# Remainders of the attention's weights on GpSimd: four instructions of 128 columns in place of one of 512

## The chip, the cores and the metric

One NeuronCore of a Trainium2 chip runs the whole program. The metric is the device time of one execution in microseconds (us); less is better. The engines are called as in the profile: PE (TensorE, the matmuls; PEld is its loading of weights), DVE (VectorE), ACT (ScalarE), POOL (GpSimd) and SP (SyncE, which issues DMAs).

## What is computed

Four layers work on x of 4 x 256 tokens with 256 features. Each adds to x an FFN of a conditioned input; the last one's FFN is a whole transformer block with attention over 16 heads of 128 and a mixture of experts. The part around the change is the attention of that layer:

```python
h = rmsnorm(x, ln1_w)
q = (h @ wq).reshape(b, s, H, HD)
k = (h @ wk).reshape(b, s, H, HD)
v = (h @ wv).reshape(b, s, H, HD)
scores = jnp.einsum('bqhd,bkhd->bhqk', q, k) / np.sqrt(HD).astype(np.float32)
scores = jnp.where(causal, scores, jnp.float32(-1000000000.0))
attn = jax.nn.softmax(scores, axis=-1)
ao = jnp.einsum('bhqk,bkhd->bqhd', attn, v).reshape(b, s, H * HD) @ wo
x = x + ao
```

## The kernel before

Activations lie with features on the 128 partitions and the 1024 tokens along the columns. The kernel is a chain of blocks, one for each stage: layer 0 (NF4 weights), layer 1 (experts chosen by sorting), layer 2 (ternary weights), the conditioning of layer 3, and `layer3`, which holds attention and experts. The order of each engine's work is written out by hand, and the engines wait for one another by counts on semaphores.

In `layer3` each product of weight and activation is taken in three passes of a reduced f32 format: high part times high part, high times low, low times high. So each weight matrix exists three times in SBUF: RAW as loaded, WH its rounded copy, WL the remainder RAW - WH; the activations as XH and XL. The attention runs over 8 groups of two heads (GROUPS). A group's weights are 4 parts of GCOL = 512 columns (for q, k, v and the output), and RAW, WH and WL have two slots, so that group g + 1 is prepared while g is computed:

- SP loads RAW of group g (L2143) once the remainders of group g - 2 are made.
- ACT rounds a part into WH (`split_high`, L2194), between its evacuations of the projections C4, C6, C8, C10 (when n is 4, 6, 8, 10, parts 0 to 3).
- POOL makes the remainder of the part (`split_low`, L2166) when ACT has counted it on w_high, and counts on w_low. POOL has nothing else to do in the groups.
- PE waits for the whole group on w_low before the first projection of it (`project`, n = 0, step D0 of the group before).

The steps of a group come from the list PLAN, read by all engines in the same order; a step's number is the unit (a head and a batch) or the projection:

```python
PLAN = """S0 C4 S1 N0 C5 C6 N1 T0 C7 S2 C8 T1 A0 N2 S3 C9 A1 T2 N3 C10 A2 T3 C11 A3
    S4 D0 S5 N4 D1 S6 N5 T4 D2 S7 N6 T5 A4 D3 N7 T6 A5 P0 T7 A6 P1 A7 W0 W1 W2 W3""".split()
```

C and D are projections: PE fills bank n % 2 (L2432 for V, L2441 for Q and K), which ACT (n even, L2209) or DVE (n odd, L2291) copies out; the next projection of the same bank waits for that. S is the scores (PE L2474, L2475), their masked row maximum on DVE (L2306, then nm at L2310) and the exponentials on ACT (L2226). N is the scaling into PN on DVE, in two instructions (L2319). T transposes PN on PE (L2482), and ACT copies the result to PT (L2234). A is the product with V (L2493, L2495), split into AH on ACT (L2242) and AL on DVE (L2325). P and W are the output projection (L2450), added to XC on DVE (L2331).

The last group makes no attention weights: POOL and ACT split the first expert's weights instead (`ex.split_low`, L1941), into the same RAW, WH and WL. The class Packed, which runs the experts, is told at which counts of w_low and wo the two slots are free. In layer 0, POOL scales HALF (L432) and multiplies EKV (L440) while DVE makes STEP (L573) and runs scans (L201, L203).

Of the kernel before, what the change touches and what calls it, by code (L numbers as in the profile page):

```python
# [13 lines left out]
F32 = mybir.dt.float32  # L14
F32R = mybir.dt.float32r
BF16 = mybir.dt.bfloat16
ALU = mybir.AluOpType
# [100 lines left out]
def chunk(t, j):  # L118

    return halves(t)[:, bass.ds(j * W, W)]  # L120
# [1511 lines left out]
GROUPS = HEADS // 2  # L1632
GCOL = 512
# [93 lines left out]
def later(g):  # L1727

    return not isinstance(g, int) or g >= 1
# [23 lines left out]
def made(g, n):  # L1753
    return LAST_MADE[n] if is_last(g) else n
# [303 lines left out]
def layer3(nc, k, io):  # L2058

    scale = float(HD) ** -0.5  # L2060
    with ExitStack() as ctx:
        def sb(name, shape, dt):
            return ctx.enter_context(nc.sbuf_tensor(name, shape, dt))

        def sem(name):
# [6 lines left out]
        RAW = sb("RAW3", [P, 2, 4 * GCOL], F32)  # L2072
        WH = sb("WH3", [P, 2, 4 * GCOL], F32R)
        WL = sb("WL3", [P, 2, 4 * GCOL], F32R)
# [28 lines left out]
        r_in, logits, rt, ex_, cw_turned, rows, sent, owned, summed, stored = [  # L2103
            sem(n + "_4") for n in ("r_in", "logits", "route", "exps", "turned", "rows", "sent", "owned", "summed", "stored")]
        ex = Packed(nc, k, sb, sem, io["l3_experts"], routed_d, (XH, XL), (RAW, WH, WL),
                    (w_low, [4 * (GROUPS - 1), 4 * GROUPS]), (wo, [4 * (GROUPS - 1), 4 * GROUPS]))

        with nc.sbuf_tensor("Q3", [P, 2, T], F32) as Q, nc.sbuf_tensor("K3", [P, 2, T], F32) as K:
            pass
# [25 lines left out]
        @block.sync  # L2135
        def _(sp):
            sp.dma_start(tiles.LN[:], io["l3_ln"]).then_inc(ln_in, 16)
            for g in range(2):
                sp.dma_start(RAW[:, g], io["l3_attn"][g]).then_inc(raw_in[g], 16)
            for g in range(2, GROUPS):  # L2140

                sp.wait_ge(w_low, 4 * (g - 1))
                sp.dma_start(RAW[:, g % 2], io["l3_attn"][g]).then_inc(raw_in[g % 2], 16)  # L2143
            sp.dma_start(RW[:], io["l3_router"]).then_inc(r_in, 16)
            sp.dma_start(routed_d[EXPERTS3:].rearrange("o (a b) -> (o a) b", b=P), k.ONES[0:T // P]).then_inc(sent, 16)
            ex.load_raw(sp, 0)
            ex.load_raw(sp, 1)

            sp.wait_ge(rows, 2)
            sp.dma_start(routed_d[0:EXPERTS3], ROWW[:]).then_inc(sent, 16)  # L2150
            sp.wait_ge(sent, 32)
            ex.load_tw(sp, 1)
            ex.load_rest(sp)
            for n, j in enumerate(ORDER):

                sp.wait_ge(summed, n + 1)
                sp.dma_start(io["out"][:, j * W:(j + 1) * W], chunk(k.X[:], j)).then_inc(stored, 16)

            sp.wait_ge(stored, 16 * NCH)

        def split_low(pool, g, slot):
            for m in range(4):

                pool.wait_ge(w_high, 4 * g + (m + 1))
                c = slice(m * GCOL, (m + 1) * GCOL)
                pool.tensor_tensor(WL[:, slot, c], RAW[:, slot, c], WH[:, slot, c].bitcast(F32),  # L2166
                                   ALU.subtract).then_inc(w_low, 1)

        @block.gpsimd
        def _(pool):  # L2170
            pool.memset(MASK[:], 0.0).then_inc(mask, 1)
            pool.wait_ge(mask, 1)

            pool.affine_select(out=MASK[:], in_=MASK[:], compare_op=ALU.is_ge, fill=NEG,
                               base=P, pattern=[[-1, 2 * P]], channel_multiplier=1).then_inc(mask, 1)
            split_low(pool, 0, 0)
            pool.memset(ex.TW[:, 0], 1.0).then_inc(ex.tw_one, 1)

            def body(g, u, r):
                if not is_last(g):  # L2180
                    split_low(pool, g + 1, 1 if u is None else u)

            each_group(pool, body)
            for part in range(3):
                ex.split_low(pool, 0, part)
            ex.gpsimd(pool)
# [220 lines left out]
        def _(pe):  # L2407
# [5 lines left out]
            def project(g, slot, n):  # L2413
                s = n % 2
                c = made(g, n)
                if n == 0:

                    pe.wait_ge(w_low, 4 * (g + 1))
                if not later(g) and n < 2:

                    pe.wait_ge(norm.xl, 2 * (n + 1))

                if n in (4, 5) and later(g):
                    pe.wait_ge(added, 4 * g - 5 + n)
                elif n >= 2 or later(g):
                    pe.wait_ge(evac[s], 6 * g + n // 2)
                if 4 <= c < 8:
                    for t in (2 * (c - 4), 2 * (c - 4) + 1):
                        passes = [(h, x, w) for h in range(KD) for x, w in ((XH, WH), (XL, WH), (XH, WL))]
                        for i, (h, x, w) in enumerate(passes):  # L2430
                            at = 2 * GCOL + h * 2 * HD
                            mm = pe.matmul(banks[s][:, (t % 2) * 2 * HD:(t % 2 + 1) * 2 * HD],  # L2432
                                           x[:, h, t * P:(t + 1) * P], w[:, slot, at:at + 2 * HD],
                                           start=(i == 0), stop=(i == len(passes) - 1))
                else:
                    head, c2 = (0, c) if c < 4 else (1, c - 8)
                    half = c2 % 2
                    passes = [(h, x, w) for h in range(KD) for x, w in ((XH, WH), (XL, WH), (XH, WL))]
                    for i, (h, x, w) in enumerate(passes):
                        at = (c2 // 2) * GCOL + (h * 2 + head) * HD  # L2440
                        mm = pe.matmul(banks[s][:], w[:, slot, at:at + HD], x[:, h, half * W:(half + 1) * W],  # L2441
                                       start=(i == 0), stop=(i == len(passes) - 1))
                mm.then_inc(proj, 1)
# [10 lines left out]
            def body(g, u, r):  # L2454
                slot = 0 if u is None else (1 + u) % 2
                for kind, n, to in steps_of(g):
# [3 lines left out]
                    if kind == "C":  # L2460
                        project(to, slot if n >= 4 else 1 - slot, n)
# [64 lines left out]
            for n in range(4):  # L2526
                project(0, 0, n)
# [44 lines left out]
def build(nc, io):  # L2572
    with ExitStack() as kept:
        k = Kit(nc)
        make_kept(nc, k, lambda name, shape, dt: kept.enter_context(nc.sbuf_tensor(name, shape, dt)))
        k.banks = [kept.enter_context(nc.psum_tensor(f"bank{i}", [P, W], F32)) for i in range(8)]
        with ExitStack() as ctx:
            make_gain(nc, k, lambda name, shape, dt: ctx.enter_context(nc.sbuf_tensor(name, shape, dt)),
                      lambda name: ctx.enter_context(nc.semaphore(name)))
            layer0(nc, k, io)  # L2580
            make_ternary(nc, k, lambda name, shape, dt: ctx.enter_context(nc.sbuf_tensor(name, shape, dt)))
            layer1(nc, k, io)
            layer2(nc, k, io)
            layer3_cond(nc, k)
        layer3(nc, k, io)
# [78 lines left out]
```

## Time and profile before

| | us |
|---|---|
| median of 3 runs | 931.06 |
| lowest and highest | 929.69, 932.71 |
| the profiled execution | 930.3 |
| its span, first to last instruction | 928.6 |
| PE busy | 777.7 (84%) |
| DVE busy | 576.0 (62%) |
| ACT busy | 415.5 (45%) |
| POOL busy | 237.6 (26%) |

The busy times are sums over the span, over stages with different limits. The attention's groups lie between about 384 and 696 us of the span. Starts in the rows below are in us from the span's start. The name in brackets behind an idle time is what ended it.

### The profile page before, as it was taken

What the parts mean: (1) busy time and instruction counts of PE and PEld (TensorE: products, weight loads), DVE (VectorE), ACT (ScalarE), POOL (GpSimd) and SP (SyncE); (2) the same over time, 40 slices, a digit from 0 to 9 for tenths busy, and PEclk for the clock granted to TensorE, in tenths of its full rate; (3) what the DMA queues carried; (4) which work ended last, traced back from release to release, by engine and by line L of the source; (5) the groups of instructions that cost most, each with busy time, mean ns of one, the idle gap of its engine ahead of it and who ended that gap; (6) DMA issues with size and microseconds to landing.
All of it is one profiled execution on the core that took longest, in us unless ns stands there. A gap on an engine that the chain in (4) does not pass through costs nothing.

```text
span 928.6 us, 11225 instructions
## 1 busy us (share of the span) xinstructions
PE 777.7 (84%) x3628; PEld 580.5 (63%) x3633; DVE 576.0 (62%) x1269; ACT 415.5 (45%) x857; POOL 237.6 (26%) x245
## 2 busy tenths in 40 slices
PE   1986695887865466999999999999979799999997
PEld 0433453544532145878788787887758688888885
DVE  6998899889989882555555556555555133332323
ACT  6894212244414555554463554635444233434332
POOL 5210101401042422102011020110102355555554
PEclk9998897889887777899999999999999999999999
DMA  4000004724120002110010110101000523224421
GB/s 144 1 1 1 0 0 173 313 64 142 40 80 0 1 1 90 46 46 22 26 47 1 46 34 14 35 1 34 1 1 1 139 62 109 57 76 95 103 52 46
DMA packets 37230, 49.84 MB, mean 54 GB/s; under 512 B 18526, under 2 KB 29894, under 8 KB 35510
## 3 DMA queue, kind: packets, MB, share of 16 engines
q1 hardware_dynamic: 36118, 46.90, 16.2%
q0 software_dynamic: 768, 2.10, 0.7%
q8 instruction: 30, 0.49, 0.2%
q14 instruction: 26, 0.21, 0.1%
q10 hardware_dynamic: 288, 0.14, 0.1%
HBM read 42.99 MB, written 6.13 MB: 53 GB/s over the span
## 4 chain that ended last, share of the span: by engine, by line
PE 47%; DVE 6%; ACT 4%; issue 2%; DMA 1%; POOL 0%; DVEq 0%; SPq 0%; ACTq 0%
PE bank L1958 15%; PE bank L1974 7%; PE bank L2441 6%; PE bank L2432 5%; PE bank L2450 4%; PE bank L2475 3%; PE bank L2493 2%; PE bank L2482 2%; PE bank L2474 1%; DVE EX L2306 1%; ACT EX L2226 1%; PE bank L2495 1%; DVE PN L2319 1%; ACT AH L2242 1%; ACT PT L2234 1%
## 5 line engine op out<-in xcount | busy, mean ns | idle before, releaser
L2013 DVE TENSOR_TENSOR B_l<-bank,TW_l 128x512 f32<-128x512 f32 (+1 forms) x50 | 34.4, 690 | 138.6 <-PE bank L1958 129.2
L2226 ACT ACTIVATE EX<-EX,nm 128x128 f32<-128x128 f32 (+1 forms) x128 | 57.5, 450 | 109.3 <-DVE nm L2310 108.6
L2046 POOL TENSOR_TENSOR HL_l<-H_l,HH_l 128x512 fp32r<-128x512 f32 (+1 forms) x50 | 65.2, 1306 | 145.1 <-ACT HH_l L2024 145.1
L2166 POOL TENSOR_TENSOR WL<-RAW,WH 128x512 fp32r<-128x512 f32 x32 | 41.0, 1287 | 228.2 <-ACT WH L2194 228.2
L1958 PE MATMUL bank<-XH,WH 128*128 128x512 f32 (+1 forms) x200 | 80.3, 401 | 3.1 <-ACT ROWW L2274 1.7
L1958 PE MATMUL bank<-XL,WH 128*128 128x512 f32 (+1 forms) x200 | 80.3, 402 | 0.0
L1958 PE MATMUL bank<-XH,WL 128*128 128x512 f32 (+1 forms) x200 | 80.2, 401 | 0.0
L2033 ACT ACTIVATE S_l<-bank 128x512 f32<-128x512 f32 (+1 forms) x50 | 29.8, 597 | 85.4 <-PE bank L1958 85.3
L2325 DVE TENSOR_TENSOR AL<-bank,AH 128x256 fp32r<-128x256 f32 x64 | 27.1, 424 | 60.6 <-ACT AH L2242 60.6
L155 POOL TENSOR_TENSOR WV<-EUK,V 128x512 f32<-128x512 f32 x16 | 23.7, 1486 | 151.8 <-DVE GAIN L244 117.0
L2441 PE MATMUL bank<-XH,WH 128*128 128x512 f32 x128 | 59.3, 463 | 1.3 <-DVE XL L1716 1.3
L1941 POOL TENSOR_TENSOR WL<-RAW,WH 128x512 fp32r<-128x512 f32 x39 | 50.7, 1300 | 32.4 <-ACT WH L1935 32.4
L2306 DVE CUSTOM_DVE_ANT_0 EX<-bank,MASK 128x128 f32<-128x128 f32 (+1 forms) x128 | 40.6, 355 | 25.6 <-PE bank L2475 25.3
L2441 PE MATMUL bank<-XH,WL 128*128 128x512 f32 x128 | 51.3, 400 | 0.0
L2441 PE MATMUL bank<-XL,WH 128*128 128x512 f32 x128 | 51.1, 399 | 0.0
L2024 ACT ACTIVATE HH_l<-H_l 128x512 fp32r<-128x512 f32 (+1 forms) x50 | 31.7, 634 | 40.8 <-PE bank L1974 34.4
L1958 PEld LDWEIGHTS bank<-XH,WH 128*128 128x128 f32 (+1 forms) x200 | 38.3, 191 | 13.1 <-ACT ROWW L2274 2.0
L474 ACT ACTIVATE MARK<-SC,THR 128x1536 bf16<-128x1536 bf16 (+1 forms) x30 | 43.1, 1512 | 6.2 <-PE bank L687 6.2
L2319 DVE TENSOR_SCALAR PN<-EX,rr 128x128 f32<-128x128 f32 (+1 forms) x128 | 43.3, 381 | 2.3
L1974 PE MATMUL bank<-HH_l,WH 128*128 128x512 f32 (+1 forms) x100 | 39.7, 397 | 5.9 <-POOL HL_l L2046 5.9
L1958 PEld LDWEIGHTS bank<-XH,WL 128*128 128x128 f32 (+1 forms) x200 | 38.2, 191 | 9.1
L1958 PEld LDWEIGHTS bank<-XL,WH 128*128 128x128 f32 (+1 forms) x200 | 38.1, 190 | 9.2
(298 smaller groups left out, 2079.3 us busy)
## 6 DMA issues: line engine op xcount, KB each, us to landing
RAW<-l_attn SPq DMA_DIRECT2D x8, 1024.0 KB, 4.8
WE<-l_experts SPq DMA_DIRECT2D x1, 6144.0 KB, 23.5
RAW<-l_experts SPq DMA_DIRECT2D x9, 512.0 KB, 3.8
TW_l<-routed SPq DMA_DIRECT2D x16, 256.0 KB, 5.1
RAW<-l_w SPq DMA_DIRECT2D x3, 1024.0 KB
TW_l<-routed SPq DMA_DIRECT2D x14, 192.0 KB, 3.1
RAW<-l_experts SPq DMA_DIRECT2D x9, 256.0 KB, 4.2
sorted_x<-ZERO SPq DMA_DIRECT2D x1, 1920.0 KB, 8.9
```

The source lines that it names most:

```text
L474: act.activation(MARK[:, n % RING, 0:cols], SC[:, at:at + cols], ACT.Sign, bias=THR[:, i:i + 1]).then_inc(mark, 1)
L1941: pool.tensor_tensor(self.WL[:, i % 2, c], self.RAW[:, i % 2, c], self.WH[:, i % 2, c].bitcast(F32), ALU.subtract).then_inc(self.w_low, 1)
L1958: mm = pe.matmul(self.k.banks[2 * (q % 2) + o][0:rows], w[:, i % 2, at:at + rows], x[:, h, n * W:(n + 1) * W], start=(s == 0), stop=(s == ...
L1974: mm = pe.matmul(self.k.banks[4 + 2 * m + n][:], w[0:rows, i % 2, at:at + P], x[0:rows, q % 4], start=((i, f, s) == (0, 0, 0)), stop=(q >= ...
L2046: pool.tensor_tensor(self.HL[0:rows, q % 4], self.H[0:rows, q % 2], self.HH[0:rows, q % 4].bitcast(F32), ALU.subtract).then_inc(self.h_low, 1)
L2166: pool.tensor_tensor(WL[:, slot, c], RAW[:, slot, c], WH[:, slot, c].bitcast(F32), ALU.subtract).then_inc(w_low, 1)
L2226: act.activation(EX[:, s, a:b], EX[:, s, a:b], ACT.Exp, bias=nm[:, s, i:i + 1], scale=scale, accum_out=rs[:, s, i:i + 1]).then_inc(expd, 1)
L2306: v.tensor_tensor_reduce(EX[:, s, a:b], banks[2 + s][:, a:b], MASK[:, 2 * P - (b - a):], 1.0, NEG, ALU.add, ALU.max, accum_out=mx[:, s, i: ...
L2319: v.tensor_scalar(PN[:, s, a:b], EX[:, s, a:b], rr[:, s, i:i + 1], None, ALU.mult).then_inc(normed, 1)
L2432: mm = pe.matmul(banks[s][:, (t % 2) * 2 * HD:(t % 2 + 1) * 2 * HD], x[:, h, t * P:(t + 1) * P], w[:, slot, at:at + 2 * HD], start=(i == 0 ...
L2441: mm = pe.matmul(banks[s][:], w[:, slot, at:at + HD], x[:, h, half * W:(half + 1) * W], start=(i == 0), stop=(i == len(passes) - 1))
L2450: mm = pe.matmul(banks[n % 2][:], w[:, slot, at:at + P], x[:, head, half * W:(half + 1) * W], start=(head == 0 and i == 0), stop=(head == ...
```

## The change

`split_low` of `layer3` goes over each part in four instructions of QCOL = 128 columns, each counting on w_low, in place of one of 512. All who wait for w_low of the attention wait for four times the count: SP's loads of RAW, PE's first projection of a group, and the experts' first loads. The experts' own `split_low` (L1941) stays with 512 columns, as do ACT's `split_high` instructions.

```diff
         ex = Packed(nc, k, sb, sem, io["l3_experts"], routed_d, (XH, XL), (RAW, WH, WL),
-                    (w_low, [4 * (GROUPS - 1), 4 * GROUPS]), (wo, [4 * (GROUPS - 1), 4 * GROUPS]))
+                    (w_low, [16 * (GROUPS - 1), 16 * GROUPS]), (wo, [4 * (GROUPS - 1), 4 * GROUPS]))
...
-                sp.wait_ge(w_low, 4 * (g - 1))
+                sp.wait_ge(w_low, 16 * (g - 1))
                 sp.dma_start(RAW[:, g % 2], io["l3_attn"][g]).then_inc(raw_in[g % 2], 16)
...
+        QCOL = GCOL // 4
+
         def split_low(pool, g, slot):
             for m in range(4):
 
                 pool.wait_ge(w_high, 4 * g + (m + 1))
-                c = slice(m * GCOL, (m + 1) * GCOL)
-                pool.tensor_tensor(WL[:, slot, c], RAW[:, slot, c], WH[:, slot, c].bitcast(F32),
-                                   ALU.subtract).then_inc(w_low, 1)
+                for at in range(m * GCOL, (m + 1) * GCOL, QCOL):
+                    c = slice(at, at + QCOL)
+                    pool.tensor_tensor(WL[:, slot, c], RAW[:, slot, c], WH[:, slot, c].bitcast(F32),
+                                       ALU.subtract).then_inc(w_low, 1)
...
                 if n == 0:
 
-                    pe.wait_ge(w_low, 4 * (g + 1))
+                    pe.wait_ge(w_low, 16 * (g + 1))
```

## Rows read from the trace of the kernel before

**Rows 1.** The page, part 1: busy time, share of span, instructions

```profile
PE 777.7 (84%) x3628; PEld 580.5 (63%) x3633; DVE 576.0 (62%) x1269; ACT 415.5 (45%) x857; POOL 237.6 (26%) x245
```

**Rows 2.** Busy time by stage, one group: PE, PEld, DVE, ACT, POOL; clock, DMA

```profile
461.00:499.50 38.50, 36.87 (x210) 31.20 (x209) 22.00 (x82) 19.10 (x60) 5.17 (x4) 1.00 0.09 29
```

**Rows 3.** Waits, 384 to 655 us: us in total, times, longest

```profile
PEld bank L2432 <- DVE V L2291: 1.8, 7, 0.3
```

**Rows 4.** Timeline of POOL and DVE, first split: start, duration, instruction [idle before]

```profile
424.15 1.29 POOL L2166 TENSOR_TENSOR WL<-RAW,WH 128x512 fp32r<-128x512 f32 x1 [24.40 <-ACT WH L2194]
...
462.65 1.29 POOL L2166 TENSOR_TENSOR WL<-RAW,WH 128x512 fp32r<-128x512 f32 x1 [24.39 <-ACT WH L2194]
...
462.72 1.56 DVE L2319 TENSOR_SCALAR PN<-EX,rr 128x128 f32<-128x128 f32 x2
464.20 0.68 DVE L2291 COPY V<-bank 128x512 f32<-128x512 f32 x1
```

**Rows 5.** Timeline of PE: T0 and C7, then T2 and C10

```profile
464.45 0.49 PE L2482 MATMUL bank<-IDF,PN 128*128 128x128 f32 x3
464.94 0.39 PE L2432 MATMUL bank<-WH,XH 128*128 128x256 f32 x1
...
472.21 0.49 PE L2482 MATMUL bank<-IDF,PN 128*128 128x128 f32 x3
472.46 0.47 PE L2441 MATMUL bank<-XH,WH 128*128 128x512 f32 x1
```

**Rows 6.** Third split: timeline of POOL, DVE, PE; then two pieces of the chain

```profile
470.27 1.30 POOL L2166 TENSOR_TENSOR WL<-RAW,WH 128x512 fp32r<-128x512 f32 x1 [3.15 <-ACT WH L2194]
...
471.41 0.55 DVE L2319 TENSOR_SCALAR PN<-EX,rr 128x128 f32<-128x128 f32 x2
...
474.44 0.70 PE L2493 MATMUL bank<-PT,V 128*128 128x256 f32 x2 [0.34 <-ACT PT L2234]
...
469.68 0.52 ACT WH L2194
...
484.47 0.45 PE bank L2475 x2
```

**Rows 7.** One line each: ns min/median/max of L2166, L1376, L432; then HALF's timeline

```profile
L2166 POOL TENSOR_TENSOR WL<-RAW,WH x32: 1263/1288/1299, 365.8 to 629.5; 128x512 fp32r<-128x512 f32 x32
...
L1376 POOL TENSOR_TENSOR H<-H,LNW x8: 2349/2362/2727, 294.7 to 330.6; 128x1024 f32<-128x1024 f32 x8
...
L432 POOL TENSOR_SCALAR HALF<-IDB x15: 528/529/542, 2.7 to 11.2; 128x128 bf16<-128x128 bf16 x15
...
2.66 9.06 POOL L432 TENSOR_SCALAR HALF<-IDB 128x128 bf16<-128x128 bf16 x15
```

**Rows 8.** Timeline of POOL and PE at the start of `layer3`

```profile
365.77 4.94 POOL L2166 TENSOR_TENSOR WL<-RAW,WH 128x512 fp32r<-128x512 f32 x4 [5.11 <-ACT WH L2194]
...
374.09 0.77 PE L2441 MATMUL bank<-XH,WH 128*128 128x512 f32 x1 [1.27 <-DVE XL L1716]
```

**Rows 9.** Timeline of POOL, DVE, PE: the second split with nm, the fourth with D0

```profile
465.85 1.28 POOL L2166 TENSOR_TENSOR WL<-RAW,WH 128x512 fp32r<-128x512 f32 x1 [1.90 <-ACT WH L2194]
...
468.00 0.17 DVE L2310 TENSOR_SCALAR nm<-mx 128x2 f32<-128x2 f32 x1
...
475.47 1.30 POOL L2166 TENSOR_TENSOR WL<-RAW,WH 128x512 fp32r<-128x512 f32 x1 [3.89 <-ACT WH L2194]
...
478.09 0.58 PE L2441 MATMUL bank<-XH,WH 128*128 128x512 f32 x1
```

**Rows 10.** Timeline of DVE and POOL in layer 0

```profile
19.23 1.70 DVE L573 TENSOR_SCALAR STEP<-SC 128x1280 bf16<-128x1280 bf16 x4
19.40 2.64 POOL L440 TENSOR_TENSOR EKV<-EK,V 128x512 f32<-128x512 f32 x1 [7.31 <-DVE EK L551]
...
23.99 1.69 DVE L203 TENSOR_TENSOR_SCAN DB<-EK,DEC 128x255 f32<-128x255 f32 x1
...
27.21 0.66 DVE L203 TENSOR_TENSOR_SCAN DB<-EK,DEC 128x255 f32<-128x255 f32 x1
```

## The prediction, made before the changed kernel was run

> **What bounds the kernel now.** I read the page's shares first, then the table by stage, then the waits, the timeline and the chain of one group, and at last the places where GpSimd and VectorE meet. The page says PE is busy for 84% of the span [rows 1], which doesn't tell what the edited stage waits for. The table by stage does: the attention's groups repeat every 38.50 us (the first splits of two groups are at 424.15 and 462.65 [rows 4]), each with 36.9 us of PE, 22.0 us of DVE and 5.2 us of POOL (four instructions), at a granted clock of 1.00 [rows 2]. PE is thus the bound, broken by small waits, and POOL has 33 us of idle time per group. POOL's own speed can matter only through (a) who waits for w_low, (b) who finds SBUF's shared access taken by it. The reader should see in the waits that nobody waits for WL in these groups (no row has POOL as the one waited for), and that one wait of 1.8 us in 7 times, PE's weight load for the V projection behind DVE's copy of V, returns once in each group 0 to 6 [rows 3].
>
> The timeline of a group shows where that comes from. POOL's first split of the group starts at 462.65 and DVE's first PN scaling at 462.72; the pair of PN instructions then takes 1.56 us [rows 4], where a pair that meets nobody takes 0.55 us [rows 6]. So DVE stands still for 1.56 - 0.55 = 1.01 us, until 1.08 us after POOL's start. That is GpSimd and VectorE excluding one another. The V copy behind the PN pair starts only at 464.20 and ends at 464.88 [rows 4]; step C7's first matmul starts at 464.94, 0.49 us after the transposes of T0, although elsewhere 0.25 us are enough between such transposes and the next matmul [rows 5]. C7 needs the bank that the V copy empties. The price of this collision on the path is therefore 0.49 - 0.25 = 0.24 us a group, not 1.01: the rest hides behind C6.
>
> From there the path runs over DVE and ACT (scores S2, row maximum, exponentials, the Q evacuation, and at 469.68 the WH split of part 2 [rows 6]), and POOL's third split starts at 470.27. PN of the third unit starts at 471.41, 1.14 us after POOL's start, and its pair takes the undisturbed 0.55 [rows 6]: it has just missed POOL. This pair is on the path: chain of PN, row maximum, nm, exponential, AH, PT, then A2 on PE at 474.44 after 0.34 us of idle PE [rows 6]. From 474.44 on the chain holds only PE's work, 18 pieces until 484.92 (the last is shown) [rows 6], so what arrives there late or early is kept.
>
> **The change, part by part.** Nothing is computed otherwise; 32 instructions of 512 columns become 128 of 128. Counts on w_low go up by four at every waiter, so every wait is for the same data.
>
> Cost of a piece. One of 512 columns takes 1.29 us at the median and 1.26 at least; one of 1024 columns (the same kind, two f32 inputs) 2.35 at least; so 2.13 ns a column [rows 7]. 384 columns fewer are 0.82 us, and a piece takes 1.29 - 0.82 = 0.47 us. Back to back the four at the stage's start go 1.22 us apart ((4.94 - 1.29) / 3) [rows 8], so pieces would go 0.40 apart. A split of four pieces lasts 3 x 0.40 + 0.47 = 1.67 us, 0.38 longer. The other end of this price is POOL's only arithmetic on 128 columns in the trace, HALF: 0.53 us each and 9.06 / 15 = 0.60 apart [rows 7]; it is bf16 with a constant, so I take the line through the two sizes of the same kind and keep 0.60 for a rival.
>
> Who waits for w_low. At the stage's start 16 pieces from 365.77 end at 365.77 + 15 x 0.40 + 0.47 = 372.24; PE's first use is at 374.09, released by XL [rows 8]: hidden, 1.8 us of cover. In a group, the last part starts at 475.47 and would end at 477.14; step D0 starts at 478.09 [rows 9]: 0.95 us of cover. SP's load of the next RAW is queued behind the same count, and so are the first two expert loads; they go 0.4 us later, and the next split of that slot comes a group (38 us) later. Behind POOL's waits only its own next pieces are queued. The second split starts at 465.85, its fourth piece would let go at about 467.31, before nm at 468.00 (467.76 after the gain below) [rows 9]. All at nothing.
>
> The first split of a group. A 512-column split keeps DVE off until 1.08 after its start, so a piece of 128 until 1.08 - 0.82 = 0.26. PN's first instruction, there at 0.07, runs at 0.26 instead of 1.08. Then it matters who is next when both queues are full. In the first stage, EKV on POOL and the scans on DVE show it: three scans in a row (one is shown) take about 1.69 us where the undisturbed one behind them takes 0.66 [rows 10]: they take turns with POOL's instructions, and each turn costs DVE 1.69 - 0.66 = 1.03 us, that is 1.03 - 0.82 = 0.21 for a piece. So PN's second instruction waits for one piece: 0.26 + 0.20 + 0.21 = 0.67 after POOL's start, 463.32, and takes 0.26 to the V copy at about 463.6. That is 0.6 us earlier than today; the copy ends 464.3, before T0's transposes end. C7 starts at 464.45 + 0.25: the whole 0.24 us is won, in 7 groups (0 to 6; the last group's splits are those of the experts and stay as they are).
>
> The third split of a group. It lets go at 1.08 today, at 3 x 0.40 + 0.26 = 1.46 afterwards. PN comes at 1.14. It finds the gap between the third piece (until 1.06) and the fourth, runs its 0.20 us, and its second instruction waits for the fourth piece: 0.21 us, on the path. Lower bound: nothing, if DVE keeps going (below). Upper bound: both pieces in full, 0.6 us. I take 0.21, from the taking of turns seen most often.
>
> Sum: 7 x (0.21 - 0.24) = -0.2 us. The profiled execution has 930.3 us (span 928.6 and 1.7 around it), so 930.1; the median of the runs shown is 0.76 above it, so 930.9.
>
> One rule of the Trainium skill speaks against the change. What the row shows first: PN at 471.41 ran at once although POOL's record lasts until 471.57, so an instruction lets go about 0.2 us before its record ends [rows 6]. The Trainium skill, SBUF — State Buffer, section "SBUF: two separate sides", says that the shared ports are held for the full instruction and that the loser fully blocks. By that rule the third split costs 0.60 instead of 0.21 and the sum would be +2.5 us. The trace agrees with the blocking, not with the last 0.2 us.
>
> **The rivals.**
> (A) DVE doesn't give way between its two PN instructions. For it: at 19.23 four STEP instructions of DVE (the same kind, one SBUF input and a constant) ran in 1.70 us with POOL's EKV already started at 19.40 and lasting 2.64 [rows 10]; POOL got in after the fourth. Against: the scans. Then the third split costs nothing: 7 x -0.24 = -1.7 us, 928.6 by the profiled execution, 929.4 by the median. The waits bound it: 1.8 us [rows 3].
> (B) Pieces shut DVE out from end to end. PN at 1.14 falls into the third piece (0.80 to 1.27), 0.13, then the fourth, 0.47: 0.60 - 0.24 = 0.36 a group, +2.5 us, 932.8 or 933.6 by the median. Against: the row at 471.41.
> (C) Slower: a POOL instruction has a floor of about 0.60 us, as HALF has. Place and price: the stage's start, where 16 pieces end at 365.77 + 15 x 0.60 + 0.53 = 375.30, 1.2 us after PE wants them; the third split, where a piece that holds 0.20 longer costs PN 0.41; and the second split, whose fourth piece (467.65 to about 468.11) meets nm at 467.76, 0.35. Together 1.2 + 7 x (0.41 + 0.35 - 0.24) = +4.8 us, 935.1 or 935.9 by the median. It decides from a spacing of about 0.52 us on: there 16 pieces reach 374.09, and the second split's last piece reaches nm. Against: the two two-input sizes leave 1.26 - 512 x 2.13 ns = 0.17 us that doesn't depend on columns [rows 7].
> (D) The change does more than the path I follow shows: DVE freed 0.6 us earlier lets later steps start earlier too. To pass 0.3% it would need 0.4 us a group; the chain offers no second wait that hangs on the first split.
>
> **How the numbers follow.** 0.3% is 2.8 us, about what a measurement of this kernel can tell from no change. Chances: forecast 0.50, A 0.22, B 0.10, C 0.10, D and the unforeseen 0.08. Faster by over 0.3% is D: 0.08. Slower is C and the upper half of B, whose 2.5 us lie just inside: 0.14. Within: 0.78. The range takes in A (929.4), the forecast and B (933.6) with a few tenths for where a median falls: 929.0 to 933.8, leaving out C and D.
>
> **What would show it.** L2166 should have 128 instructions of 0.47 us, 0.40 apart where nothing disturbs them. The first PN pair of a group should shrink from 1.56 to about 0.95, the third grow from 0.55 to about 0.76 (0.55 under A, 1.1 under B). PE's weight load for V should no longer wait for DVE's copy. The period should stay within 0.1 us of 38.50. PE at the stage's start should still be released by XL; if it is POOL, C is right. The prediction is wrong if the spacing of pieces is over 0.5 us, or if the third PN pair grows by more than a piece.

## The result, and the profile after

The changed kernel took 933.70 us (median of 9 runs, 932.13 to 936.12) beside 930.06 before: 1.0033 times the time before, 95% interval 1.002 to 1.0047. Measured twice more, in the experiments below, it was 1.0005 (0.9991 to 1.002) and 1.0024 (1.0005 to 1.0043). Two of the three intervals lie above 1 and one takes it in. So the kernel became slower rather than faster, by 0.05% to 0.33% depending on the measurement; the sign was not the one in the sum (-0.2 us), and the first measurement isn't within 0.3%. Its profiled execution has 933.19 us, span 931.5.

Where the time went is the surprise: the part that the change touches got faster. The page after, part 5, has POOL's pieces:

```profile
L2170 POOL TENSOR_TENSOR WL<-RAW,WH 128x128 fp32r<-128x128 f32 x128 | 55.1, 463 | 213.8 <-ACT WH L2198 213.8
```

0.46 us each, against 0.47 forecast. The timelines of POOL, DVE and PE around the first and the third split of the group that [rows 4 to 6] show (start, duration):

```profile
462.01 1.77 POOL L2170 TENSOR_TENSOR WL<-RAW,WH 128x128 fp32r<-128x128 f32 x4 [23.95 <-ACT WH L2198]
...
462.09 0.96 DVE L2323 TENSOR_SCALAR PN<-EX,rr 128x128 f32<-128x128 f32 x2
462.97 0.68 DVE L2295 COPY V<-bank 128x512 f32<-128x512 f32 x1
...
463.79 0.49 PE L2486 MATMUL bank<-IDF,PN 128*128 128x128 f32 x3
464.03 0.36 PE L2436 MATMUL bank<-WH,XH 128*128 128x256 f32 x1
...
469.34 1.73 POOL L2170 TENSOR_TENSOR WL<-RAW,WH 128x128 fp32r<-128x128 f32 x4 [2.45 <-ACT WH L2198]
...
470.48 0.75 DVE L2323 TENSOR_SCALAR PN<-EX,rr 128x128 f32<-128x128 f32 x2
```

The first PN pair shrank from 1.56 to 0.96 us, the third grew from 0.55 to 0.75, and C7 follows T0's transposes after 0.24 us (463.79 to 464.03) where it took 0.49. PE's wait for DVE's copy of V [rows 3] is gone from the list of waits. The next group's first split comes 38.44 us after the last's (423.57, 462.01), against 38.50. From the second group's first split to the experts' first split (seven groups; 385.65 and 655.16 before) it takes 268.75 us against 269.51: 0.11 a group, 0.76 us in all.

What lies behind the groups is the same code, and in this profile it lost 4.1 us: an ACT instruction that came 1.26 us earlier than in the profile before at 662 us (0.5 of it from the layers ahead of the attention) comes 2.86 us later at 745 us, and keeps this distance to the end. The table by stage shows why; its columns are the stretch, its length, busy us of PE, PEld, DVE, ACT and POOL with counts, the granted clock, the DMA share and GB/s. First before, then after:

```profile
660.00:700.00 40.00, 32.73 (x181) 26.55 (x181) 19.86 (x68) 17.61 (x49) 1.29 (x1) 0.96 0.00 1
700.00:750.00 50.00, 43.92 (x203) 35.77 (x203) 19.20 (x57) 19.93 (x32) 18.21 (x14) 0.93 0.27 72
```

```profile
660.00:700.00 40.00, 33.45 (x165) 27.42 (x164) 19.47 (x66) 17.70 (x49) 1.29 (x1) 0.87 0.00 1
700.00:750.00 50.00, 44.52 (x201) 36.25 (x200) 17.77 (x56) 19.05 (x31) 16.97 (x13) 0.86 0.23 65
750.00:925.00 175.00, 172.87 (x745) 139.24 (x744) 56.81 (x89) 67.48 (x115) 93.02 (x74) 1.00 0.29 74
```

TensorE's clock stands at 1.2 instead of 2.4 GHz for longer. Each microsecond at the lower level takes 0.5 off the sum, so 0.87 for 0.96 over 40 us and 0.86 for 0.93 over 50 us is 0.09 x 40 / 0.5 + 0.07 x 50 / 0.5 = 7 + 7 = 14 us more of it. The 4.1 us lie in the same two stretches. From 750 us on the two kernels run alike at 1.00. The narrower table of after and PE's timeline there show the moment:

```profile
676.00:680.00 4.00, 3.32 (x21) 3.11 (x22) 2.14 (x11) 2.44 (x7) 0.00 (x0) 0.81 0.00 0
680.00:684.00 4.00, 4.00 (x15) 3.33 (x14) 1.71 (x9) 1.90 (x7) 0.00 (x0) 0.50 0.01 2
...
676.62 0.55 PE L2486 MATMUL bank<-IDF,PN 128*128 128x128 f32 x3 [0.79 <-DVE PN L2323]
677.23 2.42 PE L1667 MATMUL bank<-ONES,SQ 128*128 128x1 f32 x16
...
681.57 1.06 PE L2497 MATMUL bank<-PT,V 128*128 128x256 f32 x2
```

Ahead of the fall PE paused for 0.79 us, did T4's transposes and began 16 matmuls of one column (the sums of squares, M0). The fall comes while they run: 0.81 over the first 4 us is 1.5 us at the lower level, and the 16 take 2.42 us where they took 1.92. From 680 to 684 it works without a gap at the lower level (0.50): the pair of matmuls at 681.57 takes 1.06 us. The kernel before has the same pause and the same sums, and kept the clock there:

```profile
677.86 0.55 PE L2482 MATMUL bank<-IDF,PN 128*128 128x128 f32 x3 [0.79 <-DVE PN L2319]
678.47 1.92 PE L1667 MATMUL bank<-ONES,SQ 128*128 128x1 f32 x16
...
681.32 0.60 PE L2493 MATMUL bank<-PT,V 128*128 128x256 f32 x2
```

### The profile page after: what moved, and what is told of

Same layout as the page of the kernel before. It is cut to its first block, busy times and chain, and to the rows that moved or that the text cites. A ratio compares the mean times of both kernels' runs of the same rounds, so it can differ in the third digit from the quotient of the medians.

```text
span 931.5 us, 11326 instructions
## 1 busy us (share of the span) xinstructions
PE 782.5 (84%) x3633; PEld 585.4 (63%) x3633; DVE 572.4 (61%) x1269; ACT 414.9 (45%) x857; POOL 251.8 (27%) x341
## 4 chain that ended last, share of the span: by engine, by line
PE 47%; DVE 5%; ACT 4%; issue 3%; DMA 1%; POOL 0%; DVEq 0%; SPq 0%; ACTq 0%
PE bank L1958 15%; PE bank L1974 7%; PE bank L2445 6%; PE bank L2436 5%; PE bank L2454 4%; PE bank L2479 3%; PE bank L2497 2%; PE bank L2486 2%; PE bank L2478 1%; DVE EX L2310 1%; DVE PN L2323 1%; ACT EX L2230 1%; PE bank L2499 1%; ACT AH L2246 1%; ACT WH L2198 1%
## 5 line engine op out<-in xcount | busy, mean ns | idle before, releaser
L2170 POOL TENSOR_TENSOR WL<-RAW,WH 128x128 fp32r<-128x128 f32 x128 | 55.1, 463 | 213.8 <-ACT WH L2198 213.8
L1941 POOL TENSOR_TENSOR WL<-RAW,WH 128x512 fp32r<-128x512 f32 x39 | 50.7, 1299 | 33.0 <-ACT WH L1935 33.0
L2497 PE MATMUL bank<-PT,V 128*128 128x256 f32 x128 | 39.9, 394 | 3.4 <-ACT PT L2238 3.4
```

The costliest lines, as they stand in the source:

```text
L1941: pool.tensor_tensor(self.WL[:, i % 2, c], self.RAW[:, i % 2, c], self.WH[:, i % 2, c].bitcast(F32), ALU.subtract).then_inc(self.w_low, 1)
L2497: pe.matmul(out[:, 0:SEQ], V[:, 2 * b, head * HD:(head + 1) * HD], PT[:, s, 0:SEQ], start=True, stop=False)
```

## The experiments

Two theories. The clock theory: all that was lost is TensorE's clock, which falls in the last group and behind it because the same pauses come at another moment. The pieces theory: the short GpSimd instructions cost the time. Ratios are to the kernel before on the same chip, with 95% intervals. Beside the time stands the mean granted clock over the executions of a kernel; 121 executions of the kernel before have 0.9264. That mean takes in the layers ahead of the attention, where the profiled executions, with the same code, spend 109 to 130 us at the lower level. So it says little about the stretch behind the groups, for which the profiles stand.

All edits are made on this form of the split (the changed kernel is `[128] * 4` for all), with the waits' counts following from it:

```diff
+def pieces_of(g, m):
+    return [128] * 4 if m == 0 and g >= 1 else [512]
...
-                c = slice(m * GCOL, (m + 1) * GCOL)
-                pool.tensor_tensor(WL[:, slot, c], RAW[:, slot, c], WH[:, slot, c].bitcast(F32),
-                                   ALU.subtract).then_inc(w_low, 1)
+                at = m * GCOL
+                for n in pieces_of(g, m):
+                    c = slice(at, at + n)
+                    pool.tensor_tensor(WL[:, slot, c], RAW[:, slot, c], WH[:, slot, c].bitcast(F32),
+                                       ALU.subtract).then_inc(w_low, 1)
+                    at += n
```

### Moving the last group in time

The hold-up is made in ScalarE's `split_high`, which the third split's place on the path makes effective at its full length; what it writes is read by nobody:

```diff
+            if m == 2:
+                at = 0
+                for n in LATE.get(g - 1, []):
+                    act.activation(halves(tiles.SQ[:])[:, at:at + n], k.ONES[:, 0:1].to_broadcast([P, n]), ACT.Copy)
+                    at += n
             act.activation(WH[:, slot, c], RAW[:, slot, c], ACT.Copy).then_inc(w_high, 1)
```

The changed kernel, with `LATE = {6: [512, 128]}`:

> The changed kernel with ScalarE held up once, by 0.72 us (two idle copies of 512 and 128 columns before the third WH split of group 6), so that the last group begins when it does in the kernel before. Clock theory (the groups got faster, and all that was lost is TensorE's clock, which falls in the last group and the first experts because this work comes 0.7 us earlier): the clock rows after the groups look as in the kernel before, and the time is that of the kernel before within 0.1%, about 930.1. Pieces theory (the short GpSimd instructions cost the time themselves): the changed kernel's 933.7 plus 0.7, about 934.4.

930.94 us, 1.0003 (0.9987 to 1.0018), mean clock 0.9268. With all 128 pieces in it and a delay added, the kernel is as fast as before. The groups' gain and the hold-up cancel (269.74 us for the seven groups), the last group's stretch is at 0.96 as before, and what lies behind the groups takes what it took before (the table at the end of this section). The time alone doesn't show that the delay did it: the unedited changed kernel wasn't measured on this chip, and on another it came to 1.0005 (below).

```profile
660.00:700.00 40.00, 32.23 (x172) 25.79 (x173) 21.11 (x72) 19.22 (x53) 2.57 (x2) 0.96 0.00 1
700.00:750.00 50.00, 44.14 (x209) 36.16 (x208) 18.64 (x57) 19.28 (x31) 17.06 (x13) 0.93 0.24 65
```

The kernel before with the same hold-up:

> The kernel before with the same hold-up of 0.72 us in group 6. Price of the hold-up alone: 930.1 + 0.7 = 930.8 if the clock after the groups stays as it was. Clock theory allows more, if 0.7 us later is also a bad moment: then the clock rows after the groups must show it. Pieces theory: 930.8, with clock rows unchanged.

930.95 us, 1.0011 (0.9995 to 1.0027), clock 0.9281; its profile has 0.96 and 0.93 in the two stretches. POOL's first split of the last group's weights, ahead of the hold-up, comes when it does in the profile before (616.65 against 616.66); the experts' first split comes 0.70 us behind it (655.86 against 655.16), and the end 0.76: the price is the delay.

Without any piece, two longer hold-ups, 1.4 us (`{6: [512, 512, 256]}`) and 2.6 us (`{5: [512, 512], 6: [512, 512, 512]}`):

> The kernel before with ScalarE held up by 1.4 us in group 6 (512, 512 and 256 idle columns). A moment between the harmless one (0.72 us) and the harmful one (2.6 us). If the harm depends on the moment: the clock rows after the groups as before (10.2 us) and 930.6 + 1.4 = 932.0, or already part of the harm; a loss that simply grows with any delay would lie on a line between 930.95 and 934.3, at 932.2, with rows in between.

932.96 us, 1.003 (1.0015 to 1.0045), clock 0.9224. The kernel before, with no piece and 1.3 us of delay (its profile: from 1.72 ahead to 0.41 ahead), ends as far above the kernel before as the changed kernel did; 1.3 us of it are the delay, and 2.2 us in the profile are lost behind the groups. Its clock:

```profile
660.00:700.00 40.00, 33.52 (x176) 27.41 (x175) 19.85 (x68) 17.66 (x49) 1.28 (x1) 0.91 0.00 1
700.00:750.00 50.00, 44.68 (x198) 36.39 (x199) 18.75 (x57) 19.35 (x32) 17.03 (x13) 0.86 0.24 65
```

> The kernel before with ScalarE held up by 5 x 0.52 = 2.6 us (two idle copies of 512 columns in group 5, three in group 6); no GpSimd piece in it. A hold-up of 0.72 us cost exactly itself, with the clock rows after the groups unchanged. If a fall of TensorE's clock depends on when the last group's pauses come, some later moment must be bad too, without any piece: then the clock rows after the groups show more time at the lower level than the 10.2 us of the kernel before, and the time is above 930.5 + 2.6 = 933.1, up to 937. Pieces theory: 933.1 and 10.2 us.

934.31 us, 1.0047 (1.0031 to 1.0062), clock 0.9245: 1.0 us over the delay itself (930.68 + 2.6 = 933.3), 1.2 by the profile, which has 0.96 and 0.86. Delays of 0.7, 1.4 and 2.6 us raise the median by 0.5, 2.5 and 3.6 us, and what their profiles lose behind the groups is 0.1, 2.2 and 1.2 us. So the loss doesn't grow with the delay, and a shift in time alone brings it, without pieces. My expectation for 1.4 us (932.0 or 932.2) was too low.

### Which pieces give and which take

> The kernel before with four pieces of 128 columns only for the first part of groups 1 to 3: 9 more GpSimd instructions in place of 96, none at the third split. The groups should gain 3 x 0.24 = 0.7 us, so that the last group begins as early as in the changed kernel. Clock theory: TensorE's clock falls in the last group as in the changed kernel, about 933.7. Pieces theory: a gain of 0.7, about 929.4.

931.13 us, 1.0009 (0.9995 to 1.0023), clock 0.9232. Between the two. The profile has the gain in the groups (0.89 us instead of 0.7) and then the fall, 0.87 from 660 to 700, with 0.93 behind, but it is the slowest of the ten executions (934.49). Nine more GpSimd instructions are enough for the fall in one execution, and 933.7 was a miss.

> The kernel before with pieces only for the first part of groups 1 to 7. The groups gain 7 x 0.24 = 1.7 us and there is no loss at the third split. If the clock after the groups were as before: 928.4. Clock theory: 928.4 plus whatever the clock rows after the groups lose against the kernel before, at 1 us for each 2 us at the lower level where TensorE works without gaps. Pieces theory: 928.4.

930.21 us, 1.0006 (0.9992 to 1.0019), clock 0.9219. The seven groups take 267.50 us against 269.51: 2.0 us faster, 0.29 each. Nothing of it arrives: 2.2 us are lost behind them. The stretches have 0.91 and 0.86. On another chip:

> Pieces for the first part of groups 1 to 7 once more. Its groups gained 2.0 us and the time was the same as before (1.0006), with a mean clock of 0.9219 over the executions. Clock theory: the same again, 930.2 to 931, clock 0.922. If the gain of 2 us arrives here (928.5), the first measurement was one of chance.

931.00 us, 1.0003 (0.9991 to 1.0015), clock 0.9242, the groups again at 267.52. It holds.

> The kernel before with four pieces only for the third part of groups 1 to 7, where PN follows 1.14 us after GpSimd's start. The groups should lose 7 x 0.21 = 1.5 us and come that much later: 932.0 if the clock after the groups is as before. The third PN pair of a group should take 0.76 us, the first 1.56 as before.

935.37 us (4 runs), 1.0063 (1.0045 to 1.0081), clock 0.9243. The pair after the third split takes 0.75, and the seven groups 270.78 us, 1.27 more, 0.18 each (0.21 forecast). The median is 3.4 us above what the groups explain (930.68 + 1.27 = 931.95). The profiled execution, the fastest of the four (932.00), accounts for 2.1 of it: that much is lost behind the groups, at 0.91 and 0.86 in the two stretches, as with the hold-up of 1.4 us, which makes the groups late by about as much (1.10). The rest isn't explained by a profile.

```profile
470.14 0.75 DVE L2334 TENSOR_SCALAR PN<-EX,rr 128x128 f32<-128x128 f32 x2
```

> Pieces only for the first group's weights, made at the stage's start (16 in place of 4), where 1.8 us of cover were forecast. Both theories: TensorE's first projection is still released by XL, and the time is that of the kernel before, 930.5, unless the clock behind the groups moves for another reason.

930.58 us, 0.9997 (0.9983 to 1.001), clock 0.9250. The stage's start costs nothing, as forecast. In the changed kernel, too, PE is released by XL there, after the same 1.27 us of idle time as in [rows 8]:

```profile
373.57 0.77 PE L2445 MATMUL bank<-XH,WH 128*128 128x512 f32 x1 [1.27 <-DVE XL L1716]
```

### Filling the pauses

Idle matmuls are put into banks that nobody uses at that time, three before T4 of the last group (its pause of 0.79 us), and in some kernels ten before W2 (the pause of 2.64 us behind the second normalisation):

```diff
                     if kind == "T":
+                        if is_last(g) and n == 4:
+                            for i in range(3):
+                                pe.matmul(banks[7][:], WH[:, slot, 0:P], WH[:, slot, 0:W], start=True, stop=True)
                         pe.wait_ge(normed, 2 * (q + 1))
...
                         else:
+                            if n == 2:
+                                for i in range(10):
+                                    pe.matmul(banks[5][:], WH[:, slot, 0:P], WH[:, slot, 0:W], start=True, stop=True)
 
                             pe.wait_ge(al, 8 * g + 8)
```

The changed kernel with the three:

> The changed kernel with three idle matmuls of 512 columns (0.23 us each, into a bank that nobody uses) on TensorE just before the transposes T4 of the last group, where it pauses for 0.79 us waiting for PN. They add work and take nothing away. Clock theory: TensorE is busier before the point where its clock fell at 678 us, so it falls there for less time or not at all: 929.5 to 931 instead of 933.7. Pieces theory: 933.7 or a little more.

929.93 us, 1.0006 (0.999 to 1.0022), clock 0.9263. In the profile it keeps 1.00 over the whole last group. That isn't yet a success of the idle matmuls: both later profiles of the changed kernel without them keep 1.00 there as well (below).

```profile
660.00:700.00 40.00, 33.43 (x191) 27.38 (x190) 19.61 (x68) 17.79 (x50) 1.28 (x1) 1.00 0.00 1
700.00:750.00 50.00, 45.78 (x209) 37.20 (x208) 20.82 (x57) 21.46 (x34) 19.71 (x16) 0.93 0.34 91
```

Pieces for the first part only, with all thirteen, on two chips:

> Pieces only for the first part of groups 1 to 7 (the groups gain 2 us), the three idle matmuls before T4, and ten more (2.3 us) in the pause of 2.64 us before W2 of the last group. Clock theory: the clock neither falls in the last group nor behind it at 693, and the gain of the groups arrives at the end: 927 to 928.5, faster than both kernels. Pieces theory has no view on the clock: 928.4 from the groups alone, with the rows of the clock as in the run with pieces for the first part.

928.00 us, 0.9974 (0.9958 to 0.9991), clock 0.9278. The fall in the last group is still there, against the expectation (0.96 from 660 to 700); what changed against the kernel without idle matmuls is the time at the lower level between 650 and 750 us, 10.2 us instead of 20.5.

> The fastest kernel so far (0.9974) once more on another chip, with pieces for the first part and idle matmuls in the last group's two pauses. Clock theory: 928 to 929, clock 0.926 to 0.928, faster than before and than the same kernel without the idle matmuls.

928.41 us, 0.9987 (0.9968 to 1.0006), clock 0.9273, beside 931.00 for the same kernel without the idle matmuls on that chip. In the tables of a short stretch, first without them, then with, both from this chip, PE stands idle for less time and the clock is 0.66 and 1.00:

```profile
688.00:692.00 4.00, 2.40 (x6) 1.92 (x7) 1.54 (x3) 0.75 (x2) 0.00 (x0) 0.66 0.00 0
```

```profile
688.00:692.00 4.00, 3.66 (x16) 2.67 (x16) 2.25 (x4) 1.50 (x3) 0.00 (x0) 1.00 0.00 0
```

This is the kernel with the lowest median of the study; the first measurement puts it below the kernel before, the second not beyond its interval. What lies behind the groups takes 3.2 and 2.8 us less than in the same kernel without idle matmuls. The two controls don't tell the same clear tale:

> The kernel before with the idle matmuls in the last group's two pauses (three before T4, ten before W2) and no piece. Clock theory: the fall behind 692 us goes or shrinks: 929.3 instead of 930.6 (3.4 us at the lower level less is about 1.4 us). Then of the 2.7 us that the run with pieces for the first part and the same idle matmuls gained, 1.3 belong to the idle matmuls and 1.4 to the pieces.

930.43 us, 1.0002 (0.9988 to 1.0017), clock 0.9254: no gain, where 1.3 us were expected. The last group ran at 1.00, but the stretch from 700 to 750 at 0.86 instead of 0.93. The time at the lower level went up from 10.2 to 13.7 us: the fall was moved, not removed.

> The changed kernel with the same idle matmuls in both pauses. Clock theory: with the clock held up in the last group, the changed kernel is faster than the filled kernel before by what its groups gain, 0.7 us: 928.6. Pieces theory: it stays 3 us behind the filled kernel before.

930.19 us, 0.9987 (0.9968 to 1.0006), clock 0.9248; 1.00 and 0.86 in the profile. It isn't 3 us behind the filled kernel before, it is level with it, and not 0.7 ahead at the median (0.7 at the mean of its executions, 929.8 to 930.5).

### The changed kernel again

> The changed kernel once more, unedited, beside the others on one chip. Clock theory: again slower than before by about 0.3% (933.5 against 930.5), with a fall of the clock in the last group around 678 us or longer falls behind it, and groups of 38.4 us. If it comes out as fast as before, the loss was one of that chip or day and the theory has little to explain.

> The changed kernel a third time. It was 1.0033 of the kernel before on one chip and 1.0005 on another. If the loss is the clock's, and how much it falls varies between executions, this one should lie between or near these two, 931 to 934, with a mean granted clock over its executions below that of the kernel before (0.9265): 0.922 with 934, 0.925 with 931. If time and clock don't go together, the clock theory is wrong.

931.26 us, 1.0005 (0.9991 to 1.002), clock 0.9248; and 933.23 us, 1.0024 (1.0005 to 1.0043), clock 0.9232. The first misses its expectation: 0.3% was expected, and nothing clear of noise came. In both, the profiled executions kept 1.00 in the last group (and 0.86 behind it) and lost only 0.5 and 0.6 us behind the groups, where the first profile lost 4.1. The second of them took 927.64 us, because the layers ahead of the attention, which the change doesn't touch, were 2.7 us faster than in the profile before.

Over the 33 executions of the changed kernel, the 8 with a mean clock of 0.926 or more took 929.6 us on average, the 14 with 0.922 or less 933.6. Of the 121 executions of the kernel before, 4 have 0.922 or less; over the others their time hardly moves with the clock (930.5 us on average below 0.925, 930.4 from there on). So the change doesn't cost a fixed time; it makes executions with a lower clock more frequent.

### The length of the groups beside the loss

One reading of the profiles goes further than the times. The table has every profile without idle matmuls, ordered by what the seven groups took (from POOL's first split for the second group to the experts' first). Beside it stands the time at 1.2 GHz between 650 and 750 us, and what lies behind the groups, from the experts' first split to the end:

| profile | seven groups, us | at 1.2 GHz, us | behind the groups, us |
|---|---|---|---|
| pieces for the first part, two chips | 267.50, 267.52 | 20.5, 20.5 | 275.6, 275.6 |
| pieces for the first part, groups 1 to 3 | 268.62 | 17.1 | 276.3 |
| the changed kernel, first profile | 268.75 | 23.9 | 277.6 |
| the changed kernel, two later ones | 269.02, 269.02 | 13.7, 13.7 | 273.9, 274.0 |
| pieces at the stage's start | 269.37 | 13.7 | 273.6 |
| the kernel before | 269.51 | 10.2 | 273.4 |
| the changed kernel, 0.7 us of delay | 269.74 | 10.2 | 273.4 |
| the kernel before, 0.7 us | 270.04 | 10.2 | 273.5 |
| the kernel before, 1.4 us | 270.61 | 20.5 | 275.6 |
| pieces for the third part | 270.78 | 20.5 | 275.5 |
| the kernel before, 2.6 us | 271.84 | 17.1 | 274.6 |

Of the 276.3 us, 0.8 are lost at the very end, where this profile alone of the table has 8 us at the lower level. The time behind the groups goes with the time at the lower level, and both go with the length of the groups, whether pieces or a delay made it. The moment in the execution doesn't seem to count by itself: the two later profiles of the changed kernel begin their second group 3.5 us apart, the kernel before and the changed one with 0.7 us of delay 2.3 us apart, and each pair agrees in both columns. Two limits: each number is from one execution, and the first profile of the changed kernel and its later ones differ by only 0.3 us in the groups, for a reason that isn't known.

## Why the prediction was wrong

Right, by its own steps, was everything inside the groups. The cost of a piece (0.47 us forecast, 0.46 measured; spacing 0.40, measured (6.64 - 0.46) / 15 = 0.41 at the stage's start). The taking of turns: the first PN pair 0.95 forecast, 0.96; the third 0.76 forecast, 0.75, so neither rival A (0.55) nor B (1.1) nor C (spacing of 0.60). The cover at the stage's start, at D0 and at nm. The gain of the first split was 0.29 us a group for 0.24 forecast, the loss at the third 0.18 for 0.21, so that the groups gained 0.76 us in the first profile (0.49 in each of the two later ones) where 0.2 were forecast. These are errors of size within the bounds given.

The step that failed is the sum. It took the groups' difference, -0.2 us, for that of the whole kernel, and so put the change behind the groups at nothing: it assumed that the last group and the experts take the same time whenever they begin. Measured, that term is +4.1 us in the first profile and +0.5 and +0.6 us in the two later ones. The prediction read the granted clock of 1.00 in the groups and didn't read on: the page's clock digits are 9 behind them, but the stretch from 660 to 750 us holds pauses of 0.79 and 2.64 us, 16 matmuls of one column, and in the kernel before already 10.2 us at 1.2 GHz (0.96 and 0.93). There was no rival for it; the 8% for the unforeseen were all placed on the faster side, and the slower rival (C) was another mechanism, which didn't happen. The range of 929.0 to 933.8 held the first median because B's bound happened to reach that far, not for its reason.

What is shown: the profiles in the table that lost over 1 us behind the groups are those with 17 us or more at the lower level there. Groups made longer without a piece bring it (1.003; 2.2 us behind the groups). The changed kernel whose groups were held up to the length of before shows none of it (273.4 us). That the short instructions cost the time themselves is refuted: the groups, which hold them, got faster, and with pieces for the first part alone a gain of 2.0 us in the groups didn't arrive at the end, on two chips.

What stays open is why one length of the groups is bad and another 0.3 us away is not; the runs give the lengths that were bad and no rule. So my clock theory was right in that the clock carries the loss, and loose in saying that the moment decides: the layers ahead of the attention vary by 5 us between the profiled executions, and that moved neither the clock behind the groups nor the loss where the groups were equally long. How often an execution turns out bad isn't known either: one execution of each measurement has a trace, and the sizes on three chips differ (0.8, 2.8 and 3.6 us by the medians). That idle matmuls help is supported for pieces in the first part alone; for the changed kernel it isn't shown, and for the one before they brought nothing.

The Trainium skill, TensorE: Matmul & The Clock Gate, section "Part 1: The HAM clock gate", says of the slow matmuls at the start of a kernel that their number varies from run to run with the phase of the activity monitor, that for a model this penalty is under 1% of a typical kernel's span, and that one shouldn't fit to a particular count. It says it of the start, and no run here measures that part alone. What these runs show is a spread between executions of one kernel on one chip from 926.7 us (clock 0.933) to 937.7 (0.918), that is 1.2%, and 0.4% between the two sets of executions above. A change worth 0.1% lies well inside that.

## What to carry to other kernels

An instruction of GpSimd on 512 columns, 1.29 us long, kept VectorE's scaling out until 1.08 us after its start. In short pieces the two take turns, which helps an operation that arrives with the first piece and hurts one that today comes just after the 1.08 us. Look for both before splitting: here pieces for the first part alone gained 0.29 us a group, pieces for the third lost 0.18. And before a gain below 0.3% is added up to the end of the kernel, read the granted clock behind the edited stage as well: here, where TensorE works with pauses, the same code ran at the other level for up to 14 us more after an edit in front of it, and in one profile that cost over five times the gain.

## What the runs showed that was not expected

What lies behind the groups, untouched by any edit in the table, took between 273.4 and 277.6 us, and two profiles of one kernel with equally long groups agree there within 0.1 us, on different chips and with starts up to 3.5 us apart. A delay of 1.4 us in the kernel before lost 2.2 us more behind it, and one of 2.6 us only 1.2. Thirteen matmuls whose result nobody reads went with 3 us less behind the groups, so that a gain of 2 us in them arrived at the end, where without them it vanished (928.4 against 931.0 us on one chip).
